# Two output pairs between the thirds of a tile's score products, and the queries' cosine product ahead of the row sums

## The chip, the cores and the metric

The kernel runs on one core of a Trainium2 chip. The core has a matrix engine (TensorE, PE in the rows; its weight loads are PEld), a vector engine (VectorE, DVE), an engine for activation functions (ScalarE, ACT), a general engine (GpSimd, POOL) and an engine that issues the DMAs (SyncE, SP). They run side by side and wait for each other through semaphores. The metric is the device time of one launch in microseconds; lower is better.

## What is computed

The input has 4 sequences of 512 tokens with 128 features. The reference runs six sublayers over it; the change lies in the third pair, which is one function run twice:

```python
x = x + 0.5 * _L0_ffn_ref(_layernorm(x), ...)
x = x + _L0_attn_ref(_layernorm(x), ...)
x = x + 0.5 * _L0_ffn_ref(_layernorm(x), ...)
x = x + 0.5 * _L1_ffn_ref(_layernorm(x), ...)   # six layers of windowed attention and feed-forward
x = x + _L1_attn_ref(_layernorm(x), ...)
x = x + 0.5 * _L1_ffn_ref(_layernorm(x), ...)   # the same again
...
def attn_layer(x, Wqkv, qs, ksc, Wo):            # 16 heads of 64, windows of 32 tokens
    ...
    q = l2norm(q) * qs
    k = l2norm(k) * ksc
    q = q * cos * scale + rotate_half(q) * sin * scale
    k = k * cos * inv + rotate_half(k) * sin * inv
    out = local_attention(q, k, v)               # each window sees itself and the one before
    return out @ Wo
```

Each of the six layers is attention and then a gated feed-forward with its own layer norm, both added to x.

## The kernel before

`windowed_layers` is called for pass 0 and pass 1. It goes through 6 layers x 16 tiles of 128 tokens (`TOTAL` = 96 steps in a pass, four tiles to a sequence), as one software pipeline. In step k, five tiles of different age are worked on: T (projected), A (one step older, normalised), B (two older, turned and scored), C (three older, probabilities and gather) and D (four older, output products). Every engine has its own function `step(s)`, and the order in which calls stand there is the order of its instructions. A loop of 32 unrolled steps runs twice in a pass.

TensorE's order in a step: `project` of the queries (L285), `turn` of tile B's queries (L291), place 0 (the feed-forward's down products, or the token transposes), output pairs 0 to 4 of tile D (`output`, L329), `turn` of B's keys, one or two more output pairs, place 1, `project` of the keys, `gather` for tile C (L321), place 2, the remaining output pairs, then `scores` for tile B (the mask at L303, written as a product into PSUM, and 64 small products at L311 that add to it), place 3. The places hold the feed-forward of a sequence, which comes round every four steps: by k % 4 it is the down and centring products (0), the broadcast of rstd or a merge of weights or a bias product (1), the gates (2) and the up products (3). A product of float32 operands is two instructions in the profile.

The PSUM tensor `ps_w` has four banks. Its first two are `ps_t`, the transposes' target; its last two are `ps_s`, the scores. The gather writes all four. ACT copies them into `px`, the last two banks first; before the mask PE waits for that first copy (`act_px`) and for the copy of the keys (`act_tk`).

DVE's order in a step: row sums of tile C's probabilities (L716) and their reciprocal (L720), cosine product (L665) and sine product (L670) of the queries of T, `feed` (L688, where there is one), transpose of the probabilities to `pT` (L731), sums of squares, cosine and sine product of the keys, maxima of B's scores (L765), subtraction. The row sums wait for exp on ACT (L573), which stands there behind the squares of the queries (L542); the cosine product waits for those squares; the keys' projection on PE waits for the sine product, since both use `ps_qk`. POOL multiplies the probabilities by the reciprocals (L863), adds cosine and sine parts (L826) and normalises (L855); `pT` waits for L863, and the gather for `pT`.

## Time and profile before

| | |
|---|---|
| median of 3 runs | 4350.42 us (4348.61 to 4353.42) |
| the profiled execution | 4346.19 us, of which the span is 4344.4 us |
| mean granted TensorE clock | 0.943 of full speed |
| PE busy | 3982.0 us, 92% |
| DVE busy | 3025.2 us, 70% |
| POOL busy | 2745.1 us, 63% |
| ACT busy | 2088.1 us, 48% |
| scores on PE (L311) | 24576 instructions, 290.7 us |
| outputs on PE (L329) | 6144 instructions, 786.1 us |

The span is the time from the first to the last instruction; the metric contains a little more. Busy shares are means over stages that differ: the two passes of windowed layers lie at about 542 to 2165 us and 2697 to 4320 us of the span. Ends of matrix products are modelled in the profile, so the distance between starts says more than the busy time. In a timeline row the columns are the start, the time, engine, line, operation, what is written and read, the count, and in brackets how long the engine had been idle and what released it.

### The profile page before, as it was taken

Reading aid. Unit: us, or ns where it says so; the run is one execution under the profiler, and the core shown is the slowest. Engines: PE = TensorE matmul, PEld = TensorE weight load, DVE = VectorE, ACT = ScalarE, POOL = GpSimd, SP = SyncE. Lnnn points to the kernel's source line nnn. Section 1 sums busy time; section 2 is a strip of 40 time slices with the busy share of each in tenths; the row PEclk is TensorE's granted clock in tenths of the full one; section 3 lists DMA queues with packets and bytes.
Section 4 is the critical chain, followed back from the end, with each engine's and each line's share of the span. In section 5 each row is a group of like instructions: output and inputs, shape, how many; then the busy total and the mean of one; then the engine's idle time right before and its main releaser. Section 6 shows DMA issues by size and latency. Waiting matters only on the chain. (4 is left out here: it accounts for less than half of the span.)

```text
span 4344.4 us, 129046 instructions
## 1 busy us (share of the span) xinstructions
PE 3982.0 (92%) x55760; PEld 2546.5 (59%) x55760; DVE 3025.2 (70%) x3477; ACT 2088.1 (48%) x2591; POOL 2745.1 (63%) x3481
## 2 busy tenths in 40 slices
PE   8999889999999999999977875899999999999997
PEld 4333456666666666666646663566666666666664
DVE  1576167878777887788744334787888788878875
ACT  2455245555555555555521112455555555555553
POOL 0000078878877888788724223888778787787873
PEclk9999989999999999999986556999999999999999
DMA  0000010000000000000000001000000000000000
GB/s 18 1 1 1 16 53 21 12 25 13 2 28 11 16 23 2 17 2 2 2 8 4 4 4 59 2 12 12 7 21 7 13 12 8 21 7 2 2 2 11
DMA packets 14548, 52.54 MB, mean 12 GB/s; under 512 B 3856, under 2 KB 6288, under 8 KB 10768
## 3 DMA queue, kind: packets, MB, share of 16 engines
q1 hardware_dynamic: 13968, 44.13, 2.9%
q8 instruction: 447, 7.32, 0.7%
q14 instruction: 133, 1.09, 0.1%
HBM read 36.78 MB, written 7.34 MB: 10 GB/s over the span
## 5 line engine op out<-in xcount | busy, mean ns | idle before, releaser
L826 POOL TENSOR_TENSOR w_qk<-w_turned 128x1024 f32<-128x1024 f32 x384 | 907.3, 2363 | 149.5 <-DVE w_turned L670 147.9
L285 PE MATMUL w_ps_qk<-w_w_qk,ZT 128*128 128x512 f32 x1536 | 767.2, 622 | 94.8 <-DVE w_turned L670 69.9
L329 PE MATMUL w_ps_y<-w_px,w_w_vo 128*128 128x128 f32 x6144 | 786.1, 276 | 2.2 <-DVE ZT L681 1.2
L329 PEld LDWEIGHTS w_ps_y<-w_px,w_w_vo 128*128 128x128 f32 x6144 | 743.1, 192 | 76.3 <-issue 73.7
L855 POOL TENSOR_TENSOR w_qk<-w_qk,w_inv_norm 128x1024 f32<-128x1024 f32 x384 | 723.0, 1904 | 0.0
L542 ACT ACTIVATE w_squares<-w_ps_qk 128x1024 f32<-128x1024 f32 x384 | 393.6, 1025 | 637.5 <-PE w_ps_qk L285 637.5
L665 DVE TENSOR_TENSOR w_turned<-w_ps_qk,w_rot_l 128x1024 f32<-128x1024 f32 x384 | 467.4, 1217 | 237.6 <-ACT w_squares L542 212.2
L863 POOL TENSOR_TENSOR w_probs<-w_probs,w_row_inv 128x1024 f32<-128x1024 f32 x192 | 365.7, 1905 | 333.1 <-DVE w_row_inv L720 332.4
L285 PEld LDWEIGHTS w_ps_qk<-w_w_qk,ZT 128*128 128x128 f32 x1536 | 282.4, 195 | 431.5 <-issue 317.2
L546 ACT ACTIVATE w_px<-w_ps_w 128x1024 f32<-128x1024 f32 x384 | 378.1, 1021 | 207.4 <-PE w_ps_w L321 207.4
L670 DVE TENSOR_TENSOR w_turned<-w_ps_qk,w_rot_l 128x1024 f32<-128x1024 f32 x384 | 466.3, 1214 | 0.0
L674 DVE TENSOR_REDUCE w_sumsq<-w_squares 128x16 f32<-128x1024 f32 x384 | 458.3, 1194 | 0.0
L291 PEld LDWEIGHTS w_ps_w<-ident,w_qk 128*128 128x128 f32 x3072 | 354.0, 142 | 115.1 <-issue 114.9
L716 DVE TENSOR_REDUCE w_row_sum<-w_probs 128x16 f32<-128x1024 f32 x192 | 234.3, 1220 | 257.5 <-ACT w_probs L573 256.9
L291 PE MATMUL w_ps_w<-ident,w_qk 128*128 128x128 f32 x3072 | 403.4, 275 | 10.6 <-ACT w_qT L578 10.6
L321 PE MATMUL w_ps_w<-w_pT,w_x_tok 32*128 32x512 f32 x3072 | 388.7, 620 | 21.9 <-DVE w_pT L731 13.5
L585 ACT ACTIVATE w_kT<-w_ps_w 128x1024 f32<-128x1024 f32 x192 | 196.8, 1025 | 343.4 <-PE w_ps_w L291 343.4
L813 POOL TENSOR_TENSOR w_rot_l<-w_rot,w_qk_scale 128x256 f32<-128x256 f32 x24 | 17.5, 731 | 532.5 <-DMA w_qk_scale<-in_qk_scale 532.5
L765 DVE TENSOR_REDUCE w_neg_max<-w_ps_w 128x16 f32<-128x1024 f32 x192 | 234.8, 1223 | 152.8 <-PE w_ps_w L311 152.8
L311 PEld LDWEIGHTS w_ps_w<-w_kT,w_qT 64*32 64x32 f32 x24576 | 255.4, 105 | 123.2 <-issue 123.2
L311 PE MATMUL w_ps_w<-w_kT,w_qT 64*32 64x64 f32 x24576 | 290.7, 225 | 37.6 <-issue 37.6
L321 PEld LDWEIGHTS w_ps_w<-w_pT,w_x_tok 32*128 32x128 f32 x3072 | 141.1, 185 | 254.1 <-issue 252.5
(273 smaller groups left out, 5950.3 us busy)
## 6 DMA issues: line engine op xcount, KB each, us to landing
w_w_qk<-in_w_qk SPq DMA_DIRECT2D x12, 1024.0 KB, 5.0
kept_w_vo<-w_w_vo SPq DMA_DIRECT2D x6, 1024.0 KB, 4.9
w_w_vo<-kept_w_vo SPq DMA_DIRECT2D x6, 1024.0 KB, 4.9
w_w<-in_w SPq DMA_DIRECT2D x12, 384.0 KB, 3.1
w_w_vT<-in_w_vT SPq DMA_DIRECT2D x6, 512.0 KB, 5.9
w_w_o<-in_w_o SPq DMA_DIRECT2D x6, 512.0 KB, 7.6
w_w<-in_w SPq DMA_DIRECT2D x12, 192.0 KB, 3.1
XT<-in_x SPq DMA_DIRECT2D x1, 1024.0 KB, 4.8
```

Source lines behind the costliest of these rows:

```text
L285: last = nc.tensor.matmul(ps_qk[:, c, :], Z[:, T.col:T.col + P], w_qk[:, T.parity, cols], start=True, stop=True)
L291: last = nc.tensor.transpose(ps_t[:, p // 4, (p % 4) * P:(p % 4 + 1) * P], qk[:, B.odd, which, p * P:(p + 1) * P], ident[:])
L311: last = nc.tensor.matmul(ps_heads[w * WIN:(w + 1) * WIN, h * PAIRS + p, :], qT[rows, p, w * WIN:(w + 1) * WIN], kT[rows, p, col:col + KEY ...
L321: last = nc.tensor.matmul(ps_w[:, w, :], x_tok[rows, C.t, half, :], pT[rows, half].rearrange("p h q -> p (h q)"), start=half == 0, stop=ha ...
L329: last = nc.tensor.matmul(ps_y[:, D.t * P:(D.t + 1) * P].rearrange("p (w q) -> p w q", q=WIN), w_vo[:, D.parity, h, p, :], px[:, D.odd, :, ...
L542: nc.scalar.activation(squares[:, which, :], flat(ps_qk[:]), ACT.Square).then_inc(act_sq, 1)
L546: nc.scalar.activation(px[:, C.odd, pair].rearrange("p w h q -> p (w h q)"), flat(ps_w[:, pair, :]), ACT.Copy).then_inc(act_px, 1)
L665: nc.vector.tensor_tensor(turned[:, which, 0, :].rearrange("p (h d) -> p h d", d=DH), flat(ps_qk[:]).rearrange("p (h d) -> p h d", d=DH), ...
L670: nc.vector.tensor_tensor(turned[:, which, 1, :].rearrange("p (h two d) -> p h two d", two=2, d=HALF), swapped, sin, ALU.mult).then_inc(dv ...
L674: nc.vector.reduce_sum(sumsq[:, which * HEADS:(which + 1) * HEADS, 0], squares[:, which, :] .rearrange("p (h d) -> p h d", d=DH), AXX).the ...
L826: nc.gpsimd.tensor_tensor(qk[:, T.odd, which, :], turned[:, which, 0, :], turned[:, which, 1, :], ALU.add).then_inc(pool_add, 1)
L855: nc.gpsimd.tensor_tensor(heads, heads, spread(inv, 2, [P, HEADS, DH]), ALU.mult).then_inc(pool_qk, 1)
```

## The change

`scores` is cut into `mask_scores` and `scores(B, pairs)`. The eight pairs of heads are scored in three groups (0 to 2, 3 to 5, 6 and 7), and output pair 6 of tile D stands between the first and the second, pair 7 between the second and the third. In steps with k % 4 of 2 and 3 pair 6 stood ahead of place 1 until now; now it never does. The wait for ACT's copy, ahead of the mask, now has no output pairs ahead of it behind place 2. On DVE `rotate` is cut into `rotate_cos` and `rotate_sin`, and for the queries the first comes ahead of the row sums, with its waits.

```diff
@@ -298,12 +298,14 @@
                     last = nc.tensor.transpose(ps_f[:, half * P:(half + 1) * P], Z[:, at:at + P], ident[:])
                 last.then_inc(pe_xt, 1)
 
-            def scores(B):
+            def mask_scores(B):
                 for a in range(2):
                     nc.tensor.matmul(ps_s[:, a, :], ident_b[:],
                                      spread(mask[:, min(B.t, 1), :], 1, [P, HEADS // 2, KEYS]),
                                      start=True, stop=False, skip_group_check=True)
-                for p in range(PAIRS):
+
+            def scores(B, pairs):
+                for p in pairs:
                     for w in range(WINS):
                         col = B.t * P + w * WIN
                         for h in range(2):
@@ -312,7 +314,7 @@
                                 ps_heads[w * WIN:(w + 1) * WIN, h * PAIRS + p, :],
                                 qT[rows, p, w * WIN:(w + 1) * WIN], kT[rows, p, col:col + KEYS],
                                 start=False, stop=True, skip_group_check=True)
-                last.then_inc(pe_s, 1)
+                return last
 
             def gather(C):
                 for half in range(2):
@@ -476,7 +478,7 @@
                     pe.wait_ge(pool_qk, B.n * 2 + 2)
                     pe.wait_ge(act_tq, B.n + 1)
                     turn(B, 1, pe_tk)
-                last_pairs = 7 if s.gate or s.up else 6
+                last_pairs = 6
                 if D:
                     output(D, range(5, last_pairs))
                 place_1(s)
@@ -491,13 +493,20 @@
                     pe.wait_ge(act_xt, C.n + 1)
                     gather(C)
                 place_2(s)
-                if D:
-                    output(D, range(last_pairs, PAIRS)).then_inc(pe_y, 1)
                 if B:
                     pe.wait_ge(act_tk, B.n + 1)
                     if C:
                         pe.wait_ge(act_px, C.n * 2 + 1)
-                    scores(B)
+                    mask_scores(B)
+                    scores(B, range(0, 3))
+                if D:
+                    output(D, (6,))
+                if B:
+                    scores(B, range(3, 6))
+                if D:
+                    output(D, (7,)).then_inc(pe_y, 1)
+                if B:
+                    scores(B, range(6, PAIRS)).then_inc(pe_s, 1)
                 place_3(s)
 
             def finish(f, prev):
@@ -657,13 +666,15 @@
             nc.vector.memset(seed[:], float(ROOT_BITS)).then_inc(edged, 1)
             dve.wait_ge(edged, run + 1)
 
-            def rotate(T, which):
+            def rotate_cos(T, which):
                 dve.wait_ge(act_sq, T.n * 2 + which + 1)
                 if T.k:
                     dve.wait_ge(pool_add, T.n * 2 + (which - 1))
                 cos = spread(rot_l[:, T.parity, which, 0, T.t, :], 1, [P, HEADS, DH])
                 nc.vector.tensor_tensor(turned[:, which, 0, :].rearrange("p (h d) -> p h d", d=DH),
                                         flat(ps_qk[:]).rearrange("p (h d) -> p h d", d=DH), cos, ALU.mult)
+
+            def rotate_sin(T, which):
                 swapped = flat(ps_qk[:]).rearrange("p (h two d) -> p h two d", two=2, d=HALF)[:, :, ::-1, :]
                 sin = spread(rot_l[:, T.parity, which, 1, T.t, :].rearrange("p (two d) -> p two d", two=2),
                              1, [P, HEADS, 2, HALF])
@@ -711,6 +722,10 @@
 
             def step(s):
                 T, A, B, C, D = s.T, s.A, s.B, s.C, s.D
+                if T:
+                    if T.k % PER == 0:
+                        dve.wait_ge(pool_rot, T.layer + 1)
+                    rotate_cos(T, 0)
                 if C:
                     dve.wait_ge(act_exp, C.n + 1)
                     nc.vector.reduce_sum(row_sum[:], probs[:], AXX).then_inc(dve_sum, 1)
@@ -719,9 +734,7 @@
                         dve.wait_ge(pool_p, C.n)
                     nc.vector.reciprocal(row_inv[:], row_sum[:]).then_inc(dve_inv, 1)
                 if T:
-                    if T.k % PER == 0:
-                        dve.wait_ge(pool_rot, T.layer + 1)
-                    rotate(T, 0)
+                    rotate_sin(T, 0)
                 if s.down:
                     feed(s.down)
                 if C:
@@ -742,7 +755,8 @@
                     nc.vector.tensor_tensor(b_h[:, parity, :], ps_f[:, 0:2 * FFB], vec[:, parity, 2:2 + 2 * FFB],
                                             ALU.add).then_inc(dve_bias, 1)
                 if T:
-                    rotate(T, 1)
+                    rotate_cos(T, 1)
+                    rotate_sin(T, 1)
                 if s.up:
                     hidden(s.up, 1)
                 if s.cen:
```

TensorE, a step with gates in the loop (k % 4 is 2), from the outputs behind the turn of the keys. `w_ps_y` is the outputs' target, `w_ps_w<-w_kT,w_qT` a score product, `w_ps_w<-mask` the mask, `w_ps_w<-w_pT` the gather, `w_ps_f<-w_xn` a gate. Before:

```order
L329 MATMUL w_ps_y<-w_px,w_w_vo 128x128 x4
L443 MATMUL w_ps_f<-w_xn,w_w 128x512
L484 REGISTER_ALU
L285 MATMUL w_ps_qk<-w_w_qk,ZT 128x512 x2
L321 MATMUL w_ps_w<-w_pT,w_x_tok 128x512 x8
L442 ISA
L443 MATMUL w_ps_f<-w_xn,w_w 128x512
L329 MATMUL w_ps_y<-w_px,w_w_vo 128x128 x2
L303 MATMUL w_ps_w<-mask,ident_b 128x512 x2
L311 MATMUL w_ps_w<-w_kT,w_qT 32x64 x64
```

After:

```order
L331 MATMUL w_ps_y<-w_px,w_w_vo 128x128 x2
L445 MATMUL w_ps_f<-w_xn,w_w 128x512
L486 REGISTER_ALU
L285 MATMUL w_ps_qk<-w_w_qk,ZT 128x512 x2
L323 MATMUL w_ps_w<-w_pT,w_x_tok 128x512 x8
L444 ISA
L445 MATMUL w_ps_f<-w_xn,w_w 128x512
L303 MATMUL w_ps_w<-mask,ident_b 128x512 x2
L313 MATMUL w_ps_w<-w_kT,w_qT 32x64 x24
L331 MATMUL w_ps_y<-w_px,w_w_vo 128x128 x2
L313 MATMUL w_ps_w<-w_kT,w_qT 32x64 x24
L331 MATMUL w_ps_y<-w_px,w_w_vo 128x128 x2
```

Two products (one pair) have left the place ahead of the first gate; they stand behind the first 24 scores, and the last pair behind the second 24.

TensorE, a step with the broadcast of rstd (k % 4 is 1, `w_ps_f<-ident,w_rstd`), from the projection of the keys to the next step's projection. Before:

```order
L285 MATMUL w_ps_qk<-w_w_qk,ZT 128x512 x2
L321 MATMUL w_ps_w<-w_pT,w_x_tok 128x512 x8
L433 REGISTER_ALU
L437 MATMUL w_ps_f<-ident,w_rstd 128x128 x4
L329 MATMUL w_ps_y<-w_px,w_w_vo 128x128 x4
L303 MATMUL w_ps_w<-mask,ident_b 128x512 x2
L311 MATMUL w_ps_w<-w_kT,w_qT 32x64 x64
L458 ISA
L285 MATMUL w_ps_qk<-w_w_qk,ZT 128x512 x2
```

After:

```order
L285 MATMUL w_ps_qk<-w_w_qk,ZT 128x512 x2
L323 MATMUL w_ps_w<-w_pT,w_x_tok 128x512 x8
L435 REGISTER_ALU
L439 MATMUL w_ps_f<-ident,w_rstd 128x128 x4
L303 MATMUL w_ps_w<-mask,ident_b 128x512 x2
L313 MATMUL w_ps_w<-w_kT,w_qT 32x64 x24
L331 MATMUL w_ps_y<-w_px,w_w_vo 128x128 x2
L313 MATMUL w_ps_w<-w_kT,w_qT 32x64 x24
L331 MATMUL w_ps_y<-w_px,w_w_vo 128x128 x2
L313 MATMUL w_ps_w<-w_kT,w_qT 32x64 x16
L460 ISA
L285 MATMUL w_ps_qk<-w_w_qk,ZT 128x512 x2
```

The four output products that stood between the broadcast and the mask are now behind it, two and two.

VectorE, the start of such a step: `w_row_sum` are the row sums, `w_turned` the cosine and then the sine product, `w_pT` the transpose. Before:

```order
L716 TENSOR_REDUCE w_row_sum<-w_probs 128x16
L720 RECIPROCAL w_row_inv<-w_row_sum 128x16
L661 ISA
L663 REGISTER_ALU
L665 TENSOR_TENSOR w_turned<-w_ps_qk,w_rot_l 128x1024
L670 TENSOR_TENSOR w_turned<-w_ps_qk,w_rot_l 128x1024
L731 STREAM_TRANSPOSE w_pT<-w_probs 128x16x2x32
```

After:

```order
L670 ISA
L672 REGISTER_ALU
L674 TENSOR_TENSOR w_turned<-w_ps_qk,w_rot_l 128x1024
L731 TENSOR_REDUCE w_row_sum<-w_probs 128x16
L735 RECIPROCAL w_row_inv<-w_row_sum 128x16
L681 TENSOR_TENSOR w_turned<-w_ps_qk,w_rot_l 128x1024
L744 STREAM_TRANSPOSE w_pT<-w_probs 128x16x2x32
```

The cosine product and its register instructions have moved ahead of the row sums; the sine product has stayed behind the reciprocal.

## Rows read from the trace of the kernel before

**Rows 1.** Stretches of four steps (kinds 3, 0, 1, 2): engines' busy us, clock
```profile
2965.22:2981.23 16.01, 15.99 (x211) 10.23 (x210) 13.40 (x15) 12.35 (x14) 12.88 (x16) 1.00 0.10 29
2981.23:2999.41 18.18, 17.70 (x221) 11.61 (x220) 15.16 (x19) 8.28 (x10) 13.77 (x19) 1.00 0.08 35
2999.41:3014.44 15.03, 13.70 (x210) 9.54 (x208) 12.02 (x12) 7.83 (x10) 12.24 (x18) 1.00 0.01 2
3014.44:3030.99 16.55, 16.04 (x216) 10.39 (x211) 13.69 (x14) 8.87 (x12) 14.79 (x19) 1.00 0.01 3
```

**Rows 2.** Timeline, head of a kind 1 step: start, us, engine, line, idle before
```profile
3001.41 1.03 ACT L542 ACTIVATE w_squares<-w_ps_qk 128x1024 f32<-128x1024 f32 x1 [1.42 <-PE w_ps_qk L285]
...
3003.42 1.22 DVE L716 TENSOR_REDUCE w_row_sum<-w_probs 128x16 f32<-128x1024 f32 x1 [1.62 <-ACT w_probs L573]
...
3004.87 1.23 DVE L665 TENSOR_TENSOR w_turned<-w_ps_qk,w_rot_l 128x1024 f32<-128x1024 f32 x1
3005.07 1.90 POOL L863 TENSOR_TENSOR w_probs<-w_probs,w_row_inv 128x1024 f32<-128x1024 f32 x1 [1.52 <-DVE w_row_inv L720]
...
3006.01 1.22 DVE L670 TENSOR_TENSOR w_turned<-w_ps_qk,w_rot_l 128x1024 f32<-128x1024 f32 x1
3007.14 1.24 DVE L731 STREAM_TRANSPOSE w_pT<-w_probs 128x1024 f32<-128x1024 f32 x1
...
3007.28 1.98 PE L285 MATMUL w_ps_qk<-w_w_qk,ZT 128*128 128x512 f32 x4 [1.33 <-DVE w_turned L670]
...
3009.19 2.00 PE L321 MATMUL w_ps_w<-w_pT,w_x_tok 32*128 32x512 f32 x16
```

**Rows 3.** Timeline, tail of the same step, from the gather's copy on
```profile
3011.26 1.94 ACT L546 ACTIVATE w_px<-w_ps_w 128x1024 f32<-128x1024 f32 x2 [0.93 <-PE w_ps_w L321]
...
3011.61 1.06 PE L329 MATMUL w_ps_y<-w_px,w_w_vo 128*128 128x128 f32 x8
...
3012.51 0.59 PE L303 MATMUL w_ps_w<-mask,ident_b 128*128 128x512 bf16 x2
...
3013.03 1.48 PE L311 MATMUL w_ps_w<-w_kT,w_qT 64*32 64x64 f32 x128
...
3014.44 0.70 PE L285 MATMUL w_ps_qk<-w_w_qk,ZT 128*128 128x512 f32 x1
```

**Rows 4.** Timeline, an early step of the second pass that has no outputs yet
```profile
2716.68 2.00 PE L321 MATMUL w_ps_w<-w_pT,w_x_tok 32*128 32x512 f32 x16
...
2719.91 0.59 PE L303 MATMUL w_ps_w<-mask,ident_b 128*128 128x512 bf16 x2 [1.24 <-ACT w_px L546]
```

**Rows 5.** Timeline, kind 1 with a merge (first), kind 0, kind 2
```profile
1515.49 1.16 PE L343 MATMUL w_ps_f<-w_w_o,w_w_vT 64*128 64x128 f32 x8
...
2985.23 1.22 DVE L716 TENSOR_REDUCE w_row_sum<-w_probs 128x16 f32<-128x1024 f32 x1 [0.25 <-ACT w_probs L573]
...
2993.38 2.00 PE L321 MATMUL w_ps_w<-w_pT,w_x_tok 32*128 32x512 f32 x16
...
2997.20 0.59 PE L303 MATMUL w_ps_w<-mask,ident_b 128*128 128x512 bf16 x2
...
3024.76 2.00 PE L321 MATMUL w_ps_w<-w_pT,w_x_tok 32*128 32x512 f32 x16
...
3028.10 0.59 PE L303 MATMUL w_ps_w<-mask,ident_b 128*128 128x512 bf16 x2
```

**Rows 6.** Timeline, single products at the scores' edges; the scores' first 0.30 us
```profile
3012.72 0.38 PE L303 MATMUL w_ps_w<-mask,ident_b 128*128 128x512 bf16 x1
...
3014.30 0.22 PE L311 MATMUL w_ps_w<-w_kT,w_qT 64*32 64x64 f32 x1
...
3013.03:3013.33 0.30, 0.30 (x33) 0.30 (x34) 1.00 0.00 0
```

**Rows 7.** Timeline, scores after a stop; the page's group of all scores
```profile
3047.89 0.33 PE L311 MATMUL w_ps_w<-w_kT,w_qT 64*32 64x64 f32 x11 [1.35 <-issue]
...
L311 PE MATMUL w_ps_w<-w_kT,w_qT 64*32 64x64 f32 x24576 | 290.7, 225 | 37.6 <-issue 37.6
```

## The prediction, made before the changed kernel was run

> **What bounds the kernel now.** The change touches only the two passes of windowed attention, 96 steps each. I read the busy time by stretch first. A run of four steps takes 65.77 us, and TensorE (PE) is busy in 15.99 of 16.01, 17.70 of 18.18, 13.70 of 15.03 and 16.04 of 16.55 us, at the full granted clock (1.00, the 2.4 GHz level), while DVE and POOL reach some 12 to 15 us [rows 1]. I call the steps kind 3, 0, 1, 2 by k % 4, in the order of these rows: kind 3 has the up products, 0 the down and centring products, 1 the broadcast of rstd, 2 the gates. So PE's own order sets the length of a step, and an edit is priced by what it does to PE's start-to-start times: an instruction moved within a step costs nothing by itself, a wait that opens or closes costs in full.
>
> Next, the timeline of a kind 1 step shows the one large wait. ACT computes the queries' squares from 3001.41 and exp behind them; DVE, idle for 1.62 us, starts the row sums at 3003.42, the cosine product at 3004.87, the sine product at 3006.01; PE, idle for 1.33 us, starts the keys' projection at 3007.28 and the gather at 3009.19 [rows 2]. Behind the gather, in the same step, PE has just enough to do: ACT copies half of `ps_w` out from 3011.26 (two copies, 1.94 us), PE meanwhile issues four output products' worth of instructions (x8) from 3011.61, the mask at 3012.51, the scores at 3013.03, and is done at 3014.44 [rows 3]. The mask writes the banks that ACT has just read, and waits for it. How tight that is shows in an early step that has no outputs yet: gather at 2716.68, mask at 2719.91, PE idle for 1.24 us until ACT's copy [rows 4]. So the mask cannot start before 3.23 us after the gather, whatever stands between. Before, it starts after 3.32 us in kind 1 [rows 2, 3], 3.34 in kind 2 and 3.82 in kind 0 [rows 5]; kind 3 is built as kind 2, and I take 3.34. The output pairs in front of the mask are the cover of that copy, and fit it to 0.1 us.
>
> **Part 1, the outputs go between the thirds of the scores.** No instruction is added. Two pairs per step (6 and 7) now stand between score products; in kinds 2 and 3 pair 6 was further up, before the gate and up products, and in kinds 0 and 1 both stood before the mask. Three terms:
>
> (a) The mask starts at 3.23 us after the gather instead of 3.82, 3.32, 3.34, 3.34 (kinds 0, 1, 2, 3): earlier by 0.59, 0.09, 0.11, 0.11.
>
> (b) Two pairs of outputs now lie between mask and end of the scores. From 3011.61 to 3012.51 they take 0.90 us [rows 3]. For (a) and (b) together PE's stretch from gather to the end of the scores grows by 0.31, 0.81, 0.79, 0.79. In kinds 0 and 1 this is all idle time of PE in front of the mask; in 2 and 3, where pair 6 comes from the head of the step, 0.45 of it is given back in part 2.
>
> (c) The split itself. Scores use a 64x32 piece of the array, outputs the whole. From the second mask product at 3012.72 to the first score is 0.31 us, while from the first mask product to the second is 0.21: 0.10 for going from whole to piece [rows 3, 6]. From the last score at 3014.30 to the next projection is 0.14, while scores follow each other every (3014.30 - 3013.03) / 127 = 0.010: 0.13 for going back [rows 3, 6]. Two splits make 2 x 0.23 = 0.46 us a step. The pause may let the queue of small instructions fill, so that the next scores start faster: after the mask, 33 of them fall into the first 0.30 us, 0.009 each against 0.010 on average [rows 3, 6]. On the 80 score instructions behind the two new pauses that is 0.08 at most, so between 0.38 and 0.46 us; I take 0.40, nearer to what the row shows of such a pause.
>
> The Trainium skill, TensorEngine Tiling (Array Packing), section Key Properties, says that changing the tiling mode, not just the tile, drains TensorE. By that rule each split costs two drains, and the page gives no size; the trace agrees, with the 0.10 and 0.13 us above. A reading of the rule without a cost would take (c) out of the sum, 77 us; that is a rival below.
>
> So the tail of the step grows by 0.71, 1.21, 1.19, 1.19 us.
>
> **Part 2, cosine ahead of the row sums, and the head of the step.** DVE waits for exp anyway, so the cosine product (1.23 us, spaced 1.14 to the next) fits into a wait of 1.62 us. In kind 1: squares end at 3002.44, cosine from 3002.48, row sums from 3003.62 (0.20 later than now), reciprocal, sine from about 3005.1, done at 3006.3 instead of 3007.23. PE's projection could start 0.9 us earlier. But the row sums' delay goes to POOL's product with the probabilities, now from 3005.07 for 1.90, then from 3005.27, and the transpose `pT` on DVE, now at 3007.14, comes at 7.34, ends at 8.58, and the gather follows 0.25 later, the distance that I estimate from the semaphore waits: 3008.83 instead of 3009.19 [rows 2]. So the head gains 0.36, not 1.33: the wait on the sine product is replaced by one on `pT`. In kind 3 the same chain binds, and I take 0.36. In kind 2 the head loses pair 6, 0.45, and `pT` is in time: 0.45. In kind 0 DVE waited only 0.25 us for exp [rows 5]; with the register work out of the way, 0.3. ACT issues nothing new, and no DMA moves. POOL gets its probabilities 0.2 us later and has some 2 us or more free in every step [rows 1].
>
> **Sum.** Kind 0: 0.71 - 0.30 = 0.41. Kind 1: 1.21 - 0.36 = 0.85. Kind 2: 1.19 - 0.45 = 0.74. Kind 3: 1.19 - 0.36 = 0.83. Four steps: +2.83 us; 48 such groups: +136 us. In ten kind 1 steps of the first pass merge products (1.16 us [rows 5]) stand before the mask, where the broadcast of kind 1 takes 3011.61 - 3009.19 - 2.00 = 0.42 [rows 2, 3]; that covers 0.7 us more of the copy: -7. One gain remains: in some steps PE stops in the middle of the scores with nothing to wait for, as at 3047.89 after 1.35 us; in the whole run 37.6 us of PE's idle time is of this kind [rows 7]. A slower stream of small instructions must shorten that, by between 0 and 37.6; the two insertions stretch the scores by 1.3 us, about one such stop, so I take 25. Total: 136 - 7 - 25 = +104 us. On the profiled execution (4346.2 us, of which the span is 4344.4) this makes 4450; on the median of the three runs, 4350.4, it makes **4454 us**.
>
> The Trainium skill, Advanced Engine Details and Errata, section ISA Cache, gives lines of 16 KB, or 256 instructions. [...] If each stop shrank by the full stretch, 37.6 would go instead of 25; no row here counts lines.
>
> **Rivals.** (1) Switching between whole and piece costs nothing, since the queue hides it: then (c) falls, 192 x 0.40 = 77 us, and the time is 4377. For it: weight loads run beside products. Against: both switches are bare where such products meet [rows 3, 6]. (2) The head gains nothing, since row sums come later and `pT` with them: kinds 0, 1 and 3 lose 0.30 + 0.36 + 0.36, times 48 is 49 us: 4503. It decides if `pT` comes 0.36 us later than I put it. (3) The other side, faster: the stops in the scores all vanish (38), the switches are free (77), and the full 1.33 us of kind 1's wait is won since `pT` keeps its place (48 x 0.97 = 47). From 4454 that takes (38 - 25) + 77 + 47 = 137, to 4317. Its place is the head of kind 1, and it needs all three; it decides where the tail grows by less than the head gives, while the wait of 1.24 us in [rows 4] says that the tail must grow by 0.3 to 0.8 even so. (4) The change does not do what it says, because the outputs' products end up elsewhere: the built order shows them where the diff puts them, so I give it nothing.
>
> **Chances and range.** The forecast 0.80, within 4420 to 4490 by its own bounds (stops 0 to 37.6, split 0.38 to 0.46, heads by 0.1 us a step). Rival 1: 0.07. Rival 2: 0.07. Rival 3: 0.06. The range from 4405 to 4495 leaves out rivals 1, 2 and 3. About 0.2% is what a measurement of this kernel can tell from no change. Faster by more than that: 0.05, most of rival 3. Within it: 0.02, the lesser forms of rival 3 and the lowest of rival 1. Slower: the other 0.93.
>
> **What would show it.** In the changed profile: PE idle before the mask with ACT's copy of `px` as its releaser in nearly every step, where [rows 4] is an exception now; gather to mask 3.23 us in all kinds; from first score to next whole-array product some 2.7 us; in kind 1 the projection after the cosine starts about 0.9 us earlier and the gather only 0.36, with idle time before the gather put down to `pT`; idle time inside the scores below 37.6 us. The prediction is wrong if the mask starts sooner than 3.2 us after the gather, if the scores with two pairs take under 2.4 us, or if the clock level in the passes changes.

## The result, and the profile after

| | before | after |
|---|---|---|
| median (4 runs each, same chip) | 4351.92 us | 4473.78 us (4472.35 to 4474.31) |
| ratio | | 1.028, 95% interval 1.026 to 1.030: slower |
| span of the profiled execution | 4344.4 us | 4470.5 us |
| mean granted TensorE clock | 0.943 | 0.947 |
| PE busy | 3982.0 us | 4109.6 us |
| DVE busy | 3025.2 us | 3018.9 us |

The change costs 122 us where +104 was forecast (4454; range 4405 to 4495). The granted clock plays no part: it is 1.00, the 2.4 GHz level, in the steps below, as in [rows 1]. First the stretches of four steps: kinds 3, 0, 1, 2 of the changed kernel. The columns are the stretch, its length, busy time of PE, PEld, DVE, ACT and POOL, the clock, DMA.

```profile
3041.65:3058.70 17.05, 16.62 (x211) 10.50 (x210) 13.50 (x15) 12.29 (x14) 13.02 (x16) 1.00 0.05 7
3058.70:3077.54 18.84, 18.52 (x222) 11.96 (x221) 15.00 (x19) 8.28 (x10) 13.54 (x19) 1.00 0.13 52
3077.54:3093.62 16.08, 14.60 (x211) 9.83 (x209) 11.94 (x12) 7.85 (x10) 12.49 (x15) 1.00 0.01 2
3093.62:3111.27 17.65, 16.86 (x220) 10.49 (x211) 13.51 (x14) 8.84 (x11) 14.71 (x21) 1.00 0.01 3
```

They take 69.62 us against 65.77. Nothing but PE has become longer.

Timeline of the head of the kind 1 step that starts at 3077.54, for [rows 2]:

```profile
3079.54 1.03 ACT L551 ACTIVATE w_squares<-w_ps_qk 128x1024 f32<-128x1024 f32 x1 [1.42 <-PE w_ps_qk L285]
...
3080.68 1.22 DVE L674 TENSOR_TENSOR w_turned<-w_ps_qk,w_rot_l 128x1024 f32<-128x1024 f32 x1 [0.74 <-ACT w_squares L551]
...
3081.83 1.21 DVE L731 TENSOR_REDUCE w_row_sum<-w_probs 128x16 f32<-128x1024 f32 x1
...
3083.24 1.16 DVE L681 TENSOR_TENSOR w_turned<-w_ps_qk,w_rot_l 128x1024 f32<-128x1024 f32 x1
...
3084.45 1.98 PE L285 MATMUL w_ps_qk<-w_w_qk,ZT 128*128 128x512 f32 x4 [0.38 <-DVE w_turned L681]
...
3085.40 1.25 DVE L744 STREAM_TRANSPOSE w_pT<-w_probs 128x1024 f32<-128x1024 f32 x1 [1.00 <-POOL w_probs L877]
...
3086.90 2.00 PE L323 MATMUL w_ps_w<-w_pT,w_x_tok 32*128 32x512 f32 x16 [0.46 <-DVE w_pT L744]
```

The cosine product (L674) fills DVE's wait for exp. The keys' projection starts 6.91 us into the step, where it was 7.87, so 0.96 earlier, and PE idles 0.38 ahead of it instead of 1.33. But the gather starts at 9.36 instead of 9.78: it now waits for `pT`, which comes at 7.86 instead of 7.73, since DVE had to wait 1.00 us for the probabilities from POOL.

The tail of the same step, for [rows 3]:

```profile
3088.95 1.94 ACT L555 ACTIVATE w_px<-w_ps_w 128x1024 f32<-128x1024 f32 x2 [1.45 <-PE w_ps_w L323]
...
3090.12 0.59 PE L303 MATMUL w_ps_w<-mask,ident_b 128*128 128x512 bf16 x2 [0.64 <-ACT w_px L555]
3090.64 0.72 PE L313 MATMUL w_ps_w<-w_kT,w_qT 64*32 64x64 f32 x48
...
3091.30 0.71 PE L331 MATMUL w_ps_y<-w_px,w_w_vo 128*128 128x128 f32 x4
...
3091.94 0.72 PE L313 MATMUL w_ps_w<-w_kT,w_qT 64*32 64x64 f32 x48
3092.59 0.71 PE L331 MATMUL w_ps_y<-w_px,w_w_vo 128*128 128x128 f32 x4
3093.23 0.45 PE L313 MATMUL w_ps_w<-w_kT,w_qT 64*32 64x64 f32 x32
3093.62 0.70 PE L285 MATMUL w_ps_qk<-w_w_qk,ZT 128*128 128x512 f32 x1
```

From gather to mask 3.22 us with 0.64 idle for ACT's copy; from first score to the next projection 2.98 us, where the scores alone took 1.41. From gather to projection: 6.72, where it was 5.25.

Two of the page's groups, and two rows of the table of waits (us in total, times, longest), for [rows 7] and the idle times in [rows 2, 4]:

```profile
L331 PE MATMUL w_ps_y<-w_px,w_w_vo 128*128 128x128 f32 x6144 | 849.1, 281 | 5.0 <-DVE ZT L692 2.7
...
L313 PE MATMUL w_ps_w<-w_kT,w_qT 64*32 64x64 f32 x24576 | 372.0, 223 | 5.4 <-issue 4.9
```

```profile
PE w_ps_w L303 <- ACT w_px L555: 61.6, 180, 1.2
...
PE w_ps_qk L285 <- DVE w_turned L681: 37.3, 43, 4.2
```

The stops in the scores ("issue": PE waits for nothing that the profile shows) have gone from 37.6 to 5.4 us, the keys' and queries' waits for the sine product from 69.9 to 37.3, and a new wait of 0.34 us on average stands before the mask in 180 of 192 steps. That new wait isn't the loss: the outputs that used to fill it now run behind it, and the loss is what they add there.

### The profile page after: what moved, and what is told of

Read it like the earlier page. It is cut to its first block and busy times, and to the rows that moved or that the text cites. A ratio compares the mean times of both kernels' runs of the same rounds, so it can differ in the third digit from the quotient of the medians.

```text
span 4470.5 us, 129046 instructions
## 1 busy us (share of the span) xinstructions
PE 4109.6 (92%) x55760; PEld 2584.6 (58%) x55760; DVE 3018.9 (68%) x3477; ACT 2085.2 (47%) x2591; POOL 2731.7 (61%) x3481
## 5 line engine op out<-in xcount | busy, mean ns | idle before, releaser
L331 PE MATMUL w_ps_y<-w_px,w_w_vo 128*128 128x128 f32 x6144 | 849.1, 281 | 5.0 <-DVE ZT L692 2.7
L285 PE MATMUL w_ps_qk<-w_w_qk,ZT 128*128 128x512 f32 x1536 | 755.1, 615 | 57.2 <-DVE w_turned L681 37.3
L674 DVE TENSOR_TENSOR w_turned<-w_ps_qk,w_rot_l 128x1024 f32<-128x1024 f32 x384 | 469.7, 1223 | 268.2 <-ACT w_squares L551 245.7
L313 PE MATMUL w_ps_w<-w_kT,w_qT 64*32 64x64 f32 x24576 | 372.0, 223 | 5.4 <-issue 4.9
L313 PEld LDWEIGHTS w_ps_w<-w_kT,w_qT 64*32 64x32 f32 x24576 | 276.3, 105 | 135.9 <-issue 89.5
L744 DVE STREAM_TRANSPOSE w_pT<-w_probs 128x1024 f32<-128x1024 f32 x192 | 239.1, 1246 | 157.4 <-POOL w_probs L877 156.0
```

Of the source, the lines that this page charges most:

```text
L285: last = nc.tensor.matmul(ps_qk[:, c, :], Z[:, T.col:T.col + P], w_qk[:, T.parity, cols], start=True, stop=True)
L313: last = nc.tensor.matmul(ps_heads[w * WIN:(w + 1) * WIN, h * PAIRS + p, :], qT[rows, p, w * WIN:(w + 1) * WIN], kT[rows, p, col:col + KEY ...
L331: last = nc.tensor.matmul(ps_y[:, D.t * P:(D.t + 1) * P].rearrange("p (w q) -> p w q", q=WIN), w_vo[:, D.parity, h, p, :], px[:, D.odd, :, ...
L674: nc.vector.tensor_tensor(turned[:, which, 0, :].rearrange("p (h d) -> p h d", d=DH), flat(ps_qk[:]).rearrange("p (h d) -> p h d", d=DH), ...
```

## Where the 122 us lie

Every step of the two traces was cut at PE's starts of the gather, the mask, the first score and what follows the last one. The last of these stretches, the scores with whatever stands between them, is called the block from here on. Medians by kind, before and after (kind 1 without merge or bias):

| kind | head: start to gather | gather to mask | block | step |
|---|---|---|---|---|
| 0 | 12.15, 11.74 | 3.82, 3.23 | 1.41, 2.98 | 18.18, 18.75 |
| 1 | 9.78, 9.37 | 3.31, 3.22 | 1.41, 2.98 | 15.02, 16.09 |
| 2 | 10.32, 9.96 | 3.34, 3.23 | 1.41, 2.98 | 16.56, 17.65 |
| 3 | 9.78, 9.37 | 3.34, 3.22 | 1.41, 2.98 | 16.02, 17.05 |

Summed over the 182 steps that can be cut so, in the prediction's terms (its own numbers worked out for 192 steps):

| term | predicted | measured |
|---|---|---|
| two pairs and two splits in the block | 1.30 x 192 = +250 | 1.564 x 182 = +284.6 |
| stops in the block, those in the outputs between the scores included | -25 | -29.5 |
| gather to mask, merges included | -43 - 7 = -50 | -45.4 |
| heads | -(0.30 + 0.36 + 0.45 + 0.36) x 48 = -71 | -83.3 |
| all the rest | 0 | -2.3 |
| sum | +104 | +124.1 |

## Experiments

Each time stands beside that of the kernel before on the same chip; diffs are against the changed kernel unless said otherwise, and `...` marks lines left out.

**The two parts apart.** `dve_only` has the new order on DVE and the old one on PE:

```diff
-                last_pairs = 6
+                last_pairs = 7 if s.gate or s.up else 6
...
+                if D:
+                    output(D, range(last_pairs, PAIRS)).then_inc(pe_y, 1)
...
                     mask_scores(B)
-                    scores(B, range(0, 3))
...
-                    scores(B, range(6, PAIRS)).then_inc(pe_s, 1)
+                    scores(B, range(PAIRS)).then_inc(pe_s, 1)
```

> TensorE's order is that of the kernel before (outputs ahead of the mask, scores in one piece); on VectorE the queries' cosine product stands ahead of the row sums, as in the changed kernel. Theory (the whole loss is in the tail of the step, and the head gains what the cosine gives): gather earlier by 0.4 us in kinds 0 and 1, 0.2 in kind 3, nothing in kind 2; 48 x 1.0 = 48 us faster than before, about 4303 us, and idle time inside the scores stays near 38 us. Rival (the later row sums, probabilities and transpose eat the gain, and the head gain of the changed kernel comes from the output pair taken out of it): 4350 us, no change.

Measured: 4310.28 us against 4345.54, ratio 0.992 (0.990 to 0.995). PE's timeline of a kind 1 step that starts at 2980.02:

```profile
2986.93 1.98 PE L285 MATMUL w_ps_qk<-w_w_qk,ZT 128*128 128x512 f32 x4 [0.38 <-DVE w_turned L675]
2989.38 2.00 PE L323 MATMUL w_ps_w<-w_pT,w_x_tok 32*128 32x512 f32 x16 [0.46 <-DVE w_pT L738]
...
2992.69 0.59 PE L303 MATMUL w_ps_w<-mask,ident_b 128*128 128x512 bf16 x2
```

The head is that of the changed kernel to 0.01 us, the mask has no wait, and the step takes 14.61. So the head's gain of 0.41 us in kind 1 belongs to the DVE edit alone. The stops in the scores are 31.9 us in this trace, 37.6 before, though nothing in the scores differs; in `dve_cen` and `filled` below they are 43.5 and 28.8. So up to some 15 us between two kernels can be stops that no edit here aims at.

`pe_only` has the new order on PE and the old one on DVE:

```diff
-                if T:
-                    if T.k % PER == 0:
-                        dve.wait_ge(pool_rot, T.layer + 1)
-                    rotate_cos(T, 0)
                 if C:
                     dve.wait_ge(act_exp, C.n + 1)
...
                 if T:
+                    if T.k % PER == 0:
+                        dve.wait_ge(pool_rot, T.layer + 1)
+                    rotate_cos(T, 0)
                     rotate_sin(T, 0)
```

> TensorE's order is that of the changed kernel, VectorE's is that of the kernel before (row sums, reciprocal, cosine, sine). Theory: the tail stays at 6.73 us; the head loses 0.4 us in kinds 0, 1 and 3, since the sine product is late again, also where the output pair was taken away: 48 x 1.2 = 57 us above the changed kernel, about 4530 us. Rival (the cosine's place is worth nothing): 4474 us.

Measured: 4531.73 us, ratio 1.042 (1.041 to 1.044), steps of 19.15, 16.51, 17.65 and 17.47 us in kinds 0 to 3. Its timeline, kind 1 from 3118.21:

```profile
3126.07 1.98 PE L285 MATMUL w_ps_qk<-w_w_qk,ZT 128*128 128x512 f32 x4 [1.32 <-DVE w_turned L681]
3127.99 2.00 PE L323 MATMUL w_ps_w<-w_pT,w_x_tok 32*128 32x512 f32 x16
```

The theory's 4530 holds, and kind 1's head is back at 9.77. The DVE edit is worth 0.8%, 33 to 35 us, with PE's old order and 1.4 to 1.5%, some 60 us, with its new one. In kinds 0 and 3 it wins 0.17 and 0.29 us in the first case and 0.40 and 0.42 in the second. In kind 3 the old order has pair 6 ahead of the gather, and PE's wait for the sine product, 0.46 us in `pe_only`, does not appear there: the pair covers it. In kind 0 both orders have both pairs behind the gather, so that this doesn't explain the difference, and it stays open. Only kind 2 gains nothing from it in either; its head gains 0.36 in `pe_only` too, by losing pair 6.

**Is it the place in the scores, or the place behind the mask?** `outs_behind` leaves both pairs behind the mask, but puts them behind the last score:

```diff
                     mask_scores(B)
-                    scores(B, range(0, 3))
+                    scores(B, range(PAIRS)).then_inc(pe_s, 1)
                 if D:
-                    output(D, (6,))
-                if B:
-                    scores(B, range(3, 6))
-                if D:
-                    output(D, (7,)).then_inc(pe_y, 1)
-                if B:
-                    scores(B, range(6, PAIRS)).then_inc(pe_s, 1)
+                    output(D, (6, 7)).then_inc(pe_y, 1)
```

> As the changed kernel, but both output pairs stand behind the last score, so that the scores are in one piece; ahead of the mask there is no pair either. Theory (each split costs by itself, 0.34 us): the gather to mask stays 3.23 us, the scores in one piece take 1.41 again, the tail with the outputs 6.06 instead of 6.73, 129 us less over 192 steps; the stops inside the scores come back in part (up to 33 us); the token transposes of kind 2 wait less since the scores end 0.9 us earlier on TensorE's clock: 4330 to 4380 us. Rival (splits are free and only the bare copy costs): 4474 us or, with the stops back, 4500. If the stops do not come back, it was the wait at the mask that removed them and not the slower scores.

Measured: 4366.58 us, ratio 1.005 (1.003 to 1.006). PE's timeline, kind 1, and the page's group of scores:

```profile
3025.39 0.59 PE L303 MATMUL w_ps_w<-mask,ident_b 128*128 128x512 bf16 x2 [0.64 <-ACT w_px L549]
3025.91 1.49 PE L313 MATMUL w_ps_w<-w_kT,w_qT 64*32 64x64 f32 x128
3027.33 1.16 PE L331 MATMUL w_ps_y<-w_px,w_w_vo 128*128 128x128 f32 x8
3028.32 0.59 PE L285 MATMUL w_ps_qk<-w_w_qk,ZT 128*128 128x512 f32 x1
```

```profile
L313 PE MATMUL w_ps_w<-w_kT,w_qT 64*32 64x64 f32 x24576 | 291.7, 226 | 44.7 <-issue 44.7
```

The wait before the mask is the same 0.64 us, yet four fifths of the loss are gone. From first score to projection it is 2.41 us with the same instructions, against 2.98: 0.57 less, 110 us in 192 steps. The stops are back (44.7 us in the scores, and 9.9 in the outputs behind them), so it isn't the mask's wait that removed them. And the heads are shorter still, by 118 us in the trace against 83. All of that lies in kinds 0 and 2 (heads of 11.39 and 9.36 us): the scores end earlier, and with them the work of DVE that hangs on them, and PE's wait of 0.60 us for the normalised rows ahead of kind 2's token transposes is gone. That the first brings about the second was not tested by itself.

By kind this run says more than its total. Beside `dve_only`, which has the pairs ahead of the mask, the steps are 0.91 us longer in kind 1 (15.52 against 14.61) and 0.65 in kind 3 (16.38 against 15.73), but shorter in kind 0 (17.78 against 18.01) and kind 2 (16.38 against 16.56). So behind the scores the pairs cost their whole 0.90 us where nothing else is gained by it, and are more than paid back where a wait in the head goes away. An order that differs by kind in this way was not run.

**How the price grows with the number of splits.** `one_split` has both pairs behind the first half of the scores:

```diff
-                    scores(B, range(0, 3))
+                    scores(B, range(0, 4))
                 if D:
-                    output(D, (6,))
+                    output(D, (6, 7)).then_inc(pe_y, 1)
                 if B:
-                    scores(B, range(3, 6))
...
+                    scores(B, range(4, PAIRS)).then_inc(pe_s, 1)
```

> As the changed kernel, but both output pairs stand together between the halves of the scores: one split instead of two. Theory: one split less, 192 x 0.34 = 65 us less than the changed kernel, about 4409 us, less a few us for stops that come back. Rival (splits are free): 4474 us.

Measured: 4427.45 us, ratio 1.019 (1.018 to 1.021), 18 us above what I had expected. Its block:

```profile
3064.76 0.86 PE L313 MATMUL w_ps_w<-w_kT,w_qT 64*32 64x64 f32 x64
3065.55 1.16 PE L331 MATMUL w_ps_y<-w_px,w_w_vo 128*128 128x128 f32 x8
3066.64 0.86 PE L313 MATMUL w_ps_w<-w_kT,w_qT 64*32 64x64 f32 x64
3067.43 0.70 PE L285 MATMUL w_ps_qk<-w_w_qk,ZT 128*128 128x512 f32 x1
```

It takes 2.67 us: 0.31 less than with two splits (60 us in 192 steps), of which 12.5 us come back as stops in the scores (17.9 in its page against 5.4). The first split costs 2.67 - 1.41 - 0.90 = 0.36, the second 0.31, not an equal 0.335 each.

`four_splits` puts the four output products one by one behind 2, 2, 2 and 1 pairs of scores (the last argument of `output` names the product of the pair; the conditions on B and D are left out here):

```diff
-                    scores(B, range(0, 3))
-                    output(D, (6,))
-                    scores(B, range(3, 6))
-                    output(D, (7,)).then_inc(pe_y, 1)
-                    scores(B, range(6, PAIRS)).then_inc(pe_s, 1)
+                    scores(B, range(0, 2))
+                    output(D, (6,), (0,))
+                    scores(B, range(2, 4))
+                    output(D, (6,), (1,))
+                    scores(B, range(4, 6))
+                    output(D, (7,), (0,))
+                    scores(B, range(6, 7))
+                    output(D, (7,), (1,)).then_inc(pe_y, 1)
+                    scores(B, range(7, PAIRS)).then_inc(pe_s, 1)
```

> As the changed kernel, but the four output products (two pairs, each pair in its halves) stand one by one between five groups of scores: four splits instead of two, with the same work. From no, one and two splits the stretch from the mask's first score to the end is 2.31 (outputs counted in), 2.67 and 2.98 us. Theory (each change between scores and outputs has its price, whatever is in between): 2.31 + 4 x 0.33 = 3.6 us, 0.65 more than with two, 192 x 0.65 = 125 us above the changed kernel, about 4599 us. Rival (the price hangs on the time that outputs take, since the queue fills or empties in it, so that two short pauses cost what a long one does): 4474 to 4500 us. Stops inside the scores stay near 5 us or fall.

Measured: 4541.59 us against 4346.99, ratio 1.045 (1.043 to 1.047). Neither expectation holds: it lies half way. Its block:

```profile
3135.85 0.46 PE L313 MATMUL w_ps_w<-w_kT,w_qT 64*32 64x64 f32 x32
3136.23 0.49 PE L331 MATMUL w_ps_y<-w_px,w_w_vo 128*128 128x128 f32 x2
3136.65 0.45 PE L313 MATMUL w_ps_w<-w_kT,w_qT 64*32 64x64 f32 x32
...
3138.26 0.34 PE L313 MATMUL w_ps_w<-w_kT,w_qT 64*32 64x64 f32 x16
3138.53 0.49 PE L331 MATMUL w_ps_y<-w_px,w_w_vo 128*128 128x128 f32 x2
3138.95 0.34 PE L313 MATMUL w_ps_w<-w_kT,w_qT 64*32 64x64 f32 x16
3139.22 0.70 PE L285 MATMUL w_ps_qk<-w_w_qk,ZT 128*128 128x512 f32 x1
```

3.37 us, 0.39 more than with two splits, so 0.195 for each further one. Start to start (medians over 182 steps) the pieces of all these kernels are these, the way into the next piece included:

| output instructions in a piece | 2 | 4 | 8 |
|---|---|---|---|
| us | 0.418 | 0.642 | 1.088 |

| score instructions in a group | 16 | 32 | 48 | 64 | 128 |
|---|---|---|---|---|---|
| us | 0.273 | 0.384 | 0.655 | 0.789 | 1.413 |

Outputs: 0.112 each and 0.194 for every insertion. Scores: 0.162 for every group and 0.007 each up to 32; what lies beyond 32 costs 0.27 for the next 16 and 0.0084 to 0.0098 each after that. So a split costs 0.194 + 0.162 = 0.356 by these lines, and gives something back if it cuts groups down to 32 or fewer.

The starts of single products show where in a split the time goes, and they are the same in every kernel with a split. Around the first piece of outputs in the changed kernel (the last score before it starts 0.146 earlier, the first score behind it at 3091.94):

```profile
3091.30 0.38 PE L331 MATMUL w_ps_y<-w_px,w_w_vo 128*128 128x128 f32 x1
...
3091.51 0.39 PE L331 MATMUL w_ps_y<-w_px,w_w_vo 128*128 128x128 f32 x2
...
3091.73 0.28 PE L331 MATMUL w_ps_y<-w_px,w_w_vo 128*128 128x128 f32 x1
```

| medians, us | in a split | otherwise | more |
|---|---|---|---|
| last score to first output | 0.146 | 0.010, score to score | 0.136 |
| first output to second | 0.213 | 0.112 | 0.101 |
| last output to first score | 0.205 | 0.112, output to output | 0.093 |

Together 0.33 for each split.

`three_splits` tests the reading of the groups, with four equal groups of 32 (the conditions on B and D are left out again):

```diff
-                    scores(B, range(0, 3))
+                    scores(B, range(0, 2))
                     output(D, (6,))
-                    scores(B, range(3, 6))
-                    output(D, (7,)).then_inc(pe_y, 1)
+                    scores(B, range(2, 4))
+                    output(D, (7,), (0,))
+                    scores(B, range(4, 6))
+                    output(D, (7,), (1,)).then_inc(pe_y, 1)
                     scores(B, range(6, PAIRS)).then_inc(pe_s, 1)
```

> The changed kernel with the scores in four equal groups of two pairs of heads; pair 6 of the outputs behind the first group, the two products of pair 7 one by one behind the second and third: three insertions instead of two, same instructions. Theory, read from the starts in the runs so far: an insertion costs 0.194 us on the outputs' side (2 instructions 0.418, 4 in 0.642, 8 in 1.088) and 0.162 on the scores' side, but a group of 32 score instructions or fewer runs at 0.007 us each (16 in 0.273, 32 in 0.384), and what lies beyond 32 in a group at 0.010 to 0.017 (48 in 0.655, 64 in 0.789, 128 in 1.413). Then from first score to the end of the last is 4 x 0.384 + 0.642 + 2 x 0.418 = 3.01 us, 0.03 more than the changed kernel's 2.98: 6 us more in the run, 4480. Rival: the third insertion costs a full 0.31 us as the second did, block 3.29, total 4533. Second rival: it costs half of what the two further ones of the kernel with four insertions cost together, (3.37 - 2.98) / 2 = 0.195, block 3.18, total 4511.

Measured: 4483.96 us against 4344.89, ratio 1.032 (1.029 to 1.035), 10 us above the changed kernel where the theory had 6 and the rivals 37 and 59. The two were timed on different chips, and by their ratios to the kernel before it is 19 us; the block, 3.02 us, is the sharper answer, where the theory had 3.01 and the rivals 3.18 and 3.29:

```profile
3097.10 0.45 PE L313 MATMUL w_ps_w<-w_kT,w_qT 64*32 64x64 f32 x32
3097.49 0.71 PE L331 MATMUL w_ps_y<-w_px,w_w_vo 128*128 128x128 f32 x4
3098.13 0.45 PE L313 MATMUL w_ps_w<-w_kT,w_qT 64*32 64x64 f32 x32
3098.51 0.49 PE L331 MATMUL w_ps_y<-w_px,w_w_vo 128*128 128x128 f32 x2
...
3099.73 0.45 PE L313 MATMUL w_ps_w<-w_kT,w_qT 64*32 64x64 f32 x32
3100.12 0.70 PE L285 MATMUL w_ps_qk<-w_w_qk,ZT 128*128 128x512 f32 x1
```

A third split costs next to nothing here, because it removes the last groups that are longer than 32 (two groups of 48 take 1.31 us, three of 32 take 1.15). Why the limit is 32 stays open: that this many instructions with their weight loads lie ready when a group begins would fit, and no run measured it.

**Which order is faster than both.** `dve_cen` is `dve_only` with pair 6 ahead of the centring products in kind 0 too, because gather to mask is 3.82 us there and the copy needs 3.23. Against `dve_only`:

```diff
-                last_pairs = 7 if s.gate or s.up else 6
+                last_pairs = 7 if s.gate or s.up or s.cen else 6
```

> The kernel with the cosine alone moved (TensorE's order as before), and in kind 0 output pair 6 ahead of the centring product, where TensorE waits 0.23 us for the feed-forward's sum, instead of behind the variances, where the copy is covered with 0.59 us to spare. Theory (a pair is free where PE waits, as long as the mask keeps 3.23 us from the gather): kind 0 shorter by 0.23 us, 48 x 0.23 = 11 us less than the kernel with the cosine alone, about 4299 us. Rival (the pair only moves the wait): 4310 us.

Measured: 4294.02 us against 4346.99, ratio 0.987 (0.986 to 0.989), as the theory had it; gather to mask in kind 0 is now 3.37, the gather itself 0.11 later than in `dve_only`, the step 17.67 where it is 18.01 there.

`filled` adds, in kind 2, pairs 0 and 1 of the outputs ahead of the token transposes, which wait there for DVE (17.8 us in the table of waits of `dve_only`). Against `dve_cen`:

```diff
                     turn(B, 0, pe_tq)
+                early = 2 if D and s.gate and s.B and s.k % TILES else 0
+                if early:
+                    pe.wait_ge(act_px, D.n * 2 + 2)
+                    output(D, range(early))
                 place_0(s)
...
-                    output(D, range(5))
+                    output(D, range(early, 5))
```

> As dve_cen, and in kind 2 output pairs 0 and 1 ahead of the token transposes, where TensorE waits 0.68 us for the normalised rows. Theory: the wait is filled with 0.90 us of work that has to be done anyway, kind 2 shorter by 0.65 us, 48 x 0.65 = 31 us less than dve_cen, about 4268 us. Rival (the transposes' later copy delays the keys' copy, or the gather then waits for pT, so that the wait moves on): 4299 us.

Measured: 4265.32 us, ratio 0.982 (0.980 to 0.984), the fastest of all and within 3 us of the theory. PE's timeline in kind 2 has no wait left in the head, and the step takes 15.83 us, where it was 16.56:

```profile
2976.76 1.04 PE L291 MATMUL w_ps_w<-ident,w_qk 128*128 128x128 f32 x8
2977.63 1.06 PE L331 MATMUL w_ps_y<-w_px,w_w_vo 128*128 128x128 f32 x8
2978.52 0.38 PE L298 MATMUL w_ps_f<-ident,ZT 128*128 128x128 f32 x2
```

## Why the prediction came out as it did

**PE's order sets the step: right.** The busy time of DVE, ACT and POOL in four steps hardly moved, and each edit on PE came out at what it did to PE's starts.

**(a) the mask at 3.23 us after the gather: right to 0.01 us,** in all four kinds. The early step without outputs [rows 4] was the right place to read it. The idle time that opened ahead of the mask is 0.25 and 0.64 us in kinds 0 and 1, less than the 0.31 and 0.81 called idle in the prediction; the starts, on which the sum rests, came out as said.

**(b) and (c), the outputs in the scores: the right mechanism, mis-sized.** The block was predicted at 2.7 us and is 2.98. The failed term is (c): 0.40 us a step, bounded by 0.38 and 0.46, where 2.98 - 1.41 - 0.90 = 0.67 was measured; over 192 steps the 0.27 make 52 us. Both edges of a split were read rightly: 0.10 for going from whole to piece is 0.093 behind an output, and 0.13 for going back is 0.136. What was left out is the second output: it starts 0.213 us after the first, not 0.112, twice a step, and that is 0.20 of the 0.27. The kernel before shows it too, where a projection follows the scores: its second product starts 0.53 us after the first (3014.44 in [rows 3] to 3014.97), and further on they follow each other every 0.43:

```profile
3014.97 1.02 PE L285 MATMUL w_ps_qk<-w_w_qk,ZT 128*128 128x512 f32 x2
```

I counted the time up to the first product behind a switch and took everything behind it to be at full rate. The rest is the 0.06 that I gave back for a queue that fills in the pause. There is such an effect, but for the first 32 of a group: cut into 48, 48 and 32, the scores together gain no more than 0.01 us on one group of 128.

The Trainium skill, TensorEngine Tiling (Array Packing), section Key Properties, has a change of the tiling mode drain TensorE. The trace agrees that such a change has a price, 0.33 us there and back, and `outs_behind` shows what it is worth: the same instructions, with two switches there and back fewer, take 0.57 us a step less. That all of it is a drain isn't shown. In the kernel before, 32 projections that start behind outputs and a wait, with no change of shape, have the same 0.53 us (median) between their first two products, so 0.10 of it looks like the price of any restart with full-size weights; no run parts the change of shape from the change of weights.

**Stops in the scores: right in direction, between the bounds.** 37.6 us fell to 5.4 in the scores, or by some 30 with the two stops that fell into outputs between them, where I took 25. Where they lie is the same in all these kernels. Stops of over 0.1 us in the block, times from the first score:

| | stops | at which product of the block | begin | end, median | us in total |
|---|---|---|---|---|---|
| before | 27 | 91st to 125th | 1.12 to 1.45 | 1.98 to 3.31, 2.71 | 37.6 |
| `outs_behind` | 36 | 98th to 133rd | 1.17 to 2.13 | 2.74 to 3.41, 3.04 | 54.6 |
| `one_split` | 41 | 98th to 133rd | 2.30 to 2.70 | 2.75 to 3.48, 2.86 | 17.7 |
| changed | 14 | 99th to 131st | 2.00 to 3.03 | 2.80 to 3.42, 3.29 | 7.4 |

A stop comes at the 91st product of the block or later, outputs counted in, whatever the groups are, and it ends mostly 2.7 to 3.4 us after the first score, whenever it began. Splits don't prevent it; they make PE reach the place later, when what it waits for has nearly come. That was the mechanism of the forecast, a slower stream that shortens the stops. The Trainium skill, Advanced Engine Details and Errata, section ISA Cache, gives lines of 256 instructions. The count of instructions is the same in `outs_behind` and in the changed kernel, and the stops are 44.7 and 5.4 us, so it isn't the number of lines alone that sets their length. Times of arrival as in the table would fit a fetch of instructions, but no run here shows what PE waits for.

**Part 2, the heads: right, a little small in kinds 0, 1 and 3.** Predicted 0.30, 0.36, 0.45, 0.36 for kinds 0 to 3, measured 0.41, 0.41, 0.36, 0.41. The projection in kind 1 is 0.96 us earlier (0.9 predicted), and the gather is held by `pT`, as predicted. `pT` is 0.13 us later, where I had put 0.20, and one step of that was wrong: POOL's product starts 0.27 us later in its step (5.93 us into it, 5.66 before), more than the 0.20 I had. But before, POOL was done at 3006.97 and `pT` started only at 3007.14 [rows 2], behind DVE's own sine product; these 0.17 us were slack that I had not counted. In kind 2 pair 6's 0.45 is not all won, since PE's wait for the normalised rows ahead of the token transposes grows from 0.51 to 0.60 us.

**Rivals.** Rival 1 (switches are free) falls with the pieces of 2.67, 2.98 and 3.37 us. Rival 2 (heads gain nothing) falls with `dve_only`, 0.8% faster. Rival 3 needed all three of its parts: one came nearly true, the stops, and the two large ones did not: switches cost more than forecast, and kind 1's head won 0.41 us, not 1.33.

**The sum.** +20 us over the forecast: +35 from the scores with their pairs (0.264 x 182 = 48, less 1.30 for each of the 10 steps that were not cut), -12 from the heads, -5 from the stops, +5 from gather to mask, -2 from the rest. The errors partly cancelled: with (c) outside its own bounds, that the time came out so near the forecast is in part luck. The answer to the change as a whole: its DVE part is a gain of 0.8% by itself, its PE part a loss of 4.2% by itself and of some 3.6% on top of the DVE part, because output pairs that filled a wait for ACT for nothing now pay their full time and two changes of the array's shape.

## What to carry to other kernels

Work that fills a wait should stay ahead of that wait; moved behind it, it costs its whole length (0.91 us a step in kind 1 of `outs_behind`), unless the move removes another wait (kinds 0 and 2 there). Products of another array shape aren't to be put into a run of small ones: each interruption here had a fixed price of 0.33 us, and it is to be read from the starts on both sides, the second product behind the switch included. And where two edits are joined, they are to be timed apart: here one was worth keeping, and became worth more with two further moves that filled waits.

## What had not been expected of the hardware

The price of an interruption has three parts: 0.14 us from the last score to the first output, 0.10 from the first output to the second, and 0.09 from the last output to the next score. Score products come at 0.007 us each for the first 32 of a group and at about 0.010 behind them, with a gap of some 0.1 us between the 32nd and the 36th, in the kernel before too. The first column of this row of the changed kernel is the stretch from the first score of a group of 32 on, and it holds all 32 in 0.25 us:

```profile
3093.23:3093.48 0.25, 0.25 (x32) 0.25 (x32) 0.00 (x0) 0.00 (x0) 1.00 0.00 0
```

And the stops "for issue" have a place and a time: never ahead of the 89th product of the block in any of the ten traces, and over 3.48 us after its first score at the latest. A block that takes 1.41 us meets them at up to 2.2 us each; one that takes about 3 us or more meets what is left of them, 6 to 7 us in the whole run.
